# A decoder layer on one Trainium2 core: the opening of cross-attention, with the token normalisation on GpSimd instead of VectorE and four weight subtractions moved later

## The reference

```python
def _layernorm(x, axis=-1, eps=1e-05):
    m = jnp.mean(x, axis=axis, keepdims=True)
    v = jnp.var(x, axis=axis, keepdims=True)
    return (x - m) / jnp.sqrt(v + eps)
...
x = x + _L0_attn_ref(_layernorm(x), ...)
x = x + _L0_xattn_ref(_layernorm(x), ctx, ctx, pos, mask, Wq, Wk, Wv, Wo)
# inside _L0_xattn_ref
q = (query @ Wq).reshape(nb, q_len, H, D).transpose(0, 2, 1, 3)
q = q * cos + _rotate_half(q) * sin
scores = jnp.where(mask == 0, -1e9, (q @ k) / sqrt(D))
x = softmax(scores) @ v ... @ Wo
```

## Time and profile before

| | |
|---|---|
| median of 3 runs | 1502.08 us |
| lowest and highest run | 1494.2 and 1506.05 us |
| the profiled execution | 1500.9 us |
| its span, first to last instruction | 1499.1 us |
| mean granted TensorE clock | 0.981 of full speed |
| busy share of PE, DVE, POOL, ACT | 96%, 73%, 32%, 28% |

### The profile page before, as it was taken

One profiled execution on the slowest core, in us unless ns is written; L12 is line 12 of the kernel. 1 busy time (PEld: TensorE's weight loads), 2 busy tenths in 40 slices (PEclk: granted clock), 3 DMA queues, 4 the chain that ended last, 5 costly groups with the idle time before them and its releaser, 6 DMA issues.

```text
span 1499.1 us, 28421 instructions
## 1 busy us (share of the span) xinstructions
PE 1442.0 (96%) x11616; PEld 1164.0 (78%) x11616; DVE 1098.8 (73%) x1632; ACT 426.1 (28%) x742; POOL 484.7 (32%) x427
## 2 busy tenths in 40 slices
PE   7999999999995699999999999999999999999999
PEld 6788888788873577877877777777778878877787
DVE  3655552888895777787787787787787887888854
ACT  4211233665652212221221222222222221221421
POOL 4322210534331233433333333333333323332221
PEclk9999999999995789999999999999999999999999
DMA  7665320000003210020010020020020020001111
GB/s 240 191 190 174 102 74 2 16 10 17 10 2 114 59 40 29 29 57 29 29 63 24 29 69 24 22 71 22 22 71 27 18 71 29 15 29 38 74 49 64
DMA packets 79121, 84.14 MB, mean 56 GB/s; under 512 B 9824, under 2 KB 50928, under 8 KB 78736
## 3 DMA queue, kind: packets, MB, share of 16 engines
q1 hardware_dynamic: 68976, 63.42, 13.4%
q10 hardware_dynamic: 9216, 16.78, 3.6%
q0 software_dynamic: 800, 2.11, 0.5%
HBM read 59.22 MB, written 23.07 MB: 55 GB/s over the span
## 4 chain that ended last, share of the span: by engine, by line
PE 64%; DVE 2%; issue 1%; ACT 1%; DMA 0%; SPq 0%; ACTq 0%
PE p_ps_q L75 9%; PE p_ps_y L1087 8%; PE p_ps_q L76 8%; PE p_ps_q L77 8%; PE p_ps_y L1088 8%; PE p_ps_y L1089 8%; PE p_ps_s L1049 4%; PE p_ps_o L1074 4%; PE p_ps_p L1059 2%; PE p_ps_y L1668 1%; PE p_ps_y L1670 1%; PE p_ps_y L1669 1%; PE p_ps_o L156 1%; PE p_ps_q L1631 0%; DMA p_raw_q<-in_wq 0%
## 5 line engine op out<-in xcount | busy, mean ns | idle before, releaser
L1395 POOL TENSOR_TENSOR p_q_rot<-p_ra,p_rb 128x512 f32<-128x512 f32 x128 | 167.0, 1304 | 289.7 <-DVE p_rb L164 289.7
L1087 PE MATMUL p_ps_y<-p_wo_hi,p_o_hi 128*128 128x512 f32 x512 | 212.2, 414 | 1.5 <-DVE p_o_lo L1282 1.4
L75 PE MATMUL p_ps_q<-p_xt_hi,p_wq_hi 128*128 128x512 f32 x512 | 212.5, 415 | 0.0
L76 PE MATMUL p_ps_q<-p_xt_lo,p_wq_hi 128*128 128x512 f32 x512 | 203.9, 398 | 0.0
L1088 PE MATMUL p_ps_y<-p_wo_lo,p_o_hi 128*128 128x512 f32 x512 | 202.7, 396 | 0.0
L77 PE MATMUL p_ps_q<-p_xt_hi,p_wq_lo 128*128 128x512 f32 x512 | 202.5, 395 | 0.0
L1089 PE MATMUL p_ps_y<-p_wo_hi,p_o_lo 128*128 128x512 f32 x512 | 202.4, 395 | 0.0
L1387 POOL TENSOR_TENSOR p_pn<-p_p,p_inv 128x512 f32<-128x512 f32 x64 | 66.9, 1045 | 301.0 <-DVE p_inv L1262 301.0
L1183 ACT ACTIVATE p_o_hi<-p_ps_o 128x512 fp32r<-128x512 f32 x128 | 69.5, 595 | 277.1 <-PE p_ps_o L1074 275.7
L1292 DVE TENSOR_TENSOR x_sb<-p_ps_y,x_sb 128x512 f32<-128x512 f32 x128 | 88.0, 688 | 78.3 <-PE p_ps_y L1089 78.3
L162 DVE TENSOR_TENSOR p_ra<-p_ps_q,p_cos_t 128x512 f32<-128x512 f32 x128 | 85.9, 671 | 62.7 <-PE p_ps_q L77 59.5
(11 more groups left out here) (217 smaller groups left out, 2992.4 us busy)
## 6 DMA issues: line engine op xcount, KB each, us to landing
p_raw_q<-in_wq SPq DMA_DIRECT2D x36, 256.0 KB, 3.2
v_scratch<-p_v_out SPq DMA_DIRECT2D x32, 256.0 KB
k_scratch<-p_k_out SPq DMA_DIRECT2D x32, 256.0 KB, 2.1
p_k_t<-k_scratch ACTq DMA_DIRECT2D x32, 256.0 KB, 2.6
p_v_in<-v_scratch ACTq DMA_DIRECT2D x32, 256.0 KB, 2.8
p_raw_o<-in_wo SPq DMA_DIRECT2D x32, 256.0 KB, 3.8
x_sb<-in_x SPq DMA_DIRECT2D x16, 256.0 KB, 2.9
out<-p_y SPq DMA_DIRECT2D x16, 256.0 KB, 2.0
```

What stands on the lines that cost most here:

```text
L75: nc.tensor.matmul(out, lh, rh, start=(c == 0), stop=False)
L76: nc.tensor.matmul(out, lh, rl, start=False, stop=False)
L1087: nc.tensor.matmul(ps_y[t][:, :], oh, w_hi["o"][h][:, :], start=(h == 0), stop=False)
L1395: nc.gpsimd.tensor_tensor(q_rot[:, h, :], ra[:, :], rb[:, :], ALU.add).then_inc(q_added, 1)
```

## The change

The normalisation of the 16 tiles moves from DVE to POOL, as `normalise_tile(t)`, with the same waits, behind a wait of POOL for the norm's mean and reciprocal root. POOL's four `split_q_lo(0, h)` and its four `add_terms(0, h)` are put between the tiles: the splits behind tiles 1, 3, 7 and 11, the additions behind tiles 9, 12 and 15 and at the end. The four `split_o_lo(0, h)` leave their place ahead of `shift(0)`; two now stand between `invert(0)` and `rotate(1, 0)`, two between `shift(1)` and `invert(1)`.

```diff
--- before.py
+++ after.py
@@ -1294,16 +1294,9 @@
                     need(dve, y_added, n * UT + t + 1)
                     norm3.collect(nc, tile + t)
 
-            def norm(t):
-                need(dve, transposed, t - 1)
-                norm2.apply(nc, xn[t % 2], t).then_inc(xn_ready, 1)
-
             norm2.finish_vector(nc, dve)
-            norm(0)
             for b in range(NB):
                 for t in range(b * TPB, (b + 1) * TPB):
-                    if t + 1 < TILES:
-                        norm(t + 1)
                     need(dve, all_hi, t + 1)
                     nc.vector.tensor_tensor(xt_lo[:, :, t * P:(t + 1) * P], ps_t[t % 2][:, :].rearrange("p (c n) -> p c n", c=KC),
                                             xt_hi[:, :, t * P:(t + 1) * P], ALU.subtract).then_inc(all_lo, 1)
@@ -1318,16 +1311,20 @@
                     dve.wait_ge(masked, 1)
                     nc.vector.tensor_scalar(bound[:, :, :], bound[:, :, :], MASKED, None, ALU.add).then_inc(masked, 1)
             rotate(0, H - 1)
-            for h in range(H):
-                split_o_lo(dve, 0, h)
             dve.wait_ge(masked, 2)
             shift(0)
             for it in range(LAST):
                 n, g, b = 2 * it, it // NB, it % NB
                 outputs_lo(n - 1)
                 invert(n)
+                if it == 0:
+                    split_o_lo(dve, 0, 0)
+                    split_o_lo(dve, 0, 1)
                 rotate(it + 1, 0)
                 shift(n + 1)
+                if it == 0:
+                    split_o_lo(dve, 0, 2)
+                    split_o_lo(dve, 0, 3)
                 add(n - 1, 0)
                 invert(n + 1)
                 rotate(it + 1, 1)
@@ -1398,11 +1395,19 @@
                 need(pool, v_part, it + 1)
                 nc.gpsimd.tensor_tensor(v_lo[:, :], v_in[:, :], v_hi[:, :], ALU.subtract).then_inc(v_ready, 1)
 
-            for w, h in (("q", 0), ("q", 1), ("q", 2), ("q", 3), ("add", 0), ("add", 1), ("add", 2), ("add", 3)):
-                if w == "add":
-                    add_terms(0, h)
-                else:
-                    split_q_lo(pool, 0, h)
+            def normalise_tile(t):
+                need(pool, transposed, t - 1)
+                nc.gpsimd.tensor_scalar(xn[t % 2], x[:, t, :], norm2.mv[:, t:t + 1, 0], norm2.rstd[:, t:t + 1],
+                                        ALU.subtract, ALU.mult).then_inc(xn_ready, 1)
+
+            pool.wait_ge(norm2.norm, norm2.root_base + 1)
+            for t in range(TILES):
+                normalise_tile(t)
+                if t in (1, 3, 7, 11):
+                    split_q_lo(pool, 0, (1, 3, 7, 11).index(t))
+                if t in (9, 12, 15):
+                    add_terms(0, (9, 12, 15).index(t))
+            add_terms(0, 3)
             for it in range(ITS):
                 n, g, b = 2 * it, it // NB, it % NB
                 normalise_p(n)
```

## The result

| | before | after |
|---|---|---|
| median | 1498.2 us | 1511.37 us |
| profiled execution | 1500.9 us | 1509.43 us |
| ratio, with 95% interval | | 1.008 [1.0058, 1.0102] |

The change makes the kernel slower by 0.8%, some 12 us. One of the ten executions of each kernel lies far outside the others (6682.77 us before, 2027.31 us after, that one at 0.652 of the clock) and is left out of the ratio. The forecast was 1504.5, range 1496 to 1510, and "no change that can be measured". The direction of the sum was right (+2.4), its size was not. In the profiled executions the span grew from 1499.1 to 1507.6 us, by 8.5; the profiled execution of before was itself 2.7 above the median of its longer series.

What follows compares the result with a forecast made beforehand. PE was taken to bound the kernel, the change being worth what it moves mix(0). Terms 0 + 0.9 - 0.5 + 1.4 + 0.55 gave +2.35, say +2.4 us: median about 1504.5, range 1496 to 1510.

Steps and rivals of the forecast that it cites:

- What bounds the kernel: PE, busy 853.28 of 855.00 us after 545; a delay reaching it by then is carried to the end one for one.
- The price of the operation, 1.04 us: POOL's two-step normalisation of one 128x512 tile, taken from its broadcast multiply at 1.045; ends 0.52 and 1.26 us.
- Tiles 0 to 7, nothing: First eight normalisations on POOL: no loss, since PE's cadence of 1.13 us isn't shorter than 1.04; lead taken as 0.
- Tiles 8 to 11, +0.9: POOL's split waits for ACT ahead of tile 8; tile 11 +0.4 us at the high clock or +1.4 at the low.
- tile 13, still +0.9: POOL's head 1 addition, queued ahead, waits for the rotation and meets the mask; tile 13 +0.4 to +1.4 us, middle +0.9.
- Output weights: Four subtractions leaving shift(0): -0.5 us; first pair before rotate(1, 0): +1.4; second ahead of invert(1): +0.55.
- The queues: SP's loads of mask and weights start or land later but still before their use; nothing lost.
- The third rival: POOL's chain to tile 15, 484.0 + 16 d, decides from d = 1.75 us; 1512.5 at d = 2.30; chance 0.07.

Runs made afterwards that it cites:

- e3_pool_multiply: Changed kernel, same order, but POOL's operation per tile is one broadcast multiply by the reciprocal root, mean subtraction left out; 1.0031 of before.
- e4_four_forms: Changed kernel with four forms of POOL's operation, one or two steps, per-token scalars or constants, four tiles each; 2.07, 1.55, 1.91, 1.50 us, no kernel time claimed.
- e2_weights_only: Kernel before with only the four output-weight subtractions moved as in the change, normalisation still on DVE; 1.0027 of before.
- the control: Kernel before with one further wait on POOL for the norm's reciprocal, meant to move nothing in the opening; 0.9995 of before.
- e10_weights_free_place: Kernel before with only the four output-weight subtractions moved between outputs_lo(0) and rotate(1, 3); 1.0037 of before.
- e6_pool_order: Changed kernel with head 2's and 3's weight splits behind tiles 8 and 9, head 0's and 1's additions behind 10 and 14; scores(0) at 50.98, no time claimed.
- e9_reordered_dve: Kernel before, tiles 5, 9, 13 normalised ahead of rotations, mask behind rotate(0, 3), output-weight subtractions between outputs_lo(0) and rotate(1, 3); 0.9979 of before.

## Why the prediction was wrong, step by step

- **What bounds the kernel:** right. Nothing behind the opening changed (948.2 against 948.2), and what PE had lost at scores(2), 9.9 us, arrived at the end one for one.
- **The price of the operation, 1.04 us: wrong, and it is the step that failed.** 2.07 was measured, above the 1.75 that the prediction itself gave as a sign of being wrong. It was taken from the nearest row by size and by reading a broadcast, and both ends of its range, 0.52 and 1.26, came from other kinds of instruction. The range of the sum was made from these ends and so was too narrow. `e3_pool_multiply` shows that with the assumed price the first part costs nothing, and `e4_four_forms` which part of the price belongs to what.
- **Tiles 0 to 7, nothing:** wrong, and it follows from the price. PE came to tile 7 at 19.44 from the reciprocal, against 14.82 before: +4.6.
- **Tiles 8 to 11, +0.9, and tile 13, still +0.9:** the waits were where the prediction had them, for ACT ahead of tile 8 and for the rotation ahead of tile 13. Their size: tile 11 was 9.1 late (32.21 against 23.12), tile 13 10.7 (42.14 against 31.44). With the cheap form both were 0 and not +0.9: tile 11 stood at 23.05 and tile 13 at 31.42, so that not even the better end of the two clocks, +0.4, came true. Even with the right price these two terms were too dear.
- **Output weights:** the removal was to give -0.5 at scores(0). The addition of head 3 took 1.26 in `e2_weights_only`, as assumed, and 1.76 before. The landmark scores(0) alone doesn't show it, since the control has 45.14 too, with the subtractions in their old place; but from tile 15 to scores(0) it was 9.90 before, 9.87 in the control and 9.39 in `e2_weights_only`. The two pairs cost 1.52 at mix(0) (16.37 us from scores(0) before, 17.89 after; 1.96 against the control's 15.93), against 1.4 + 0.55. The first took 2.09 beside POOL, against 1.25 + 0.9. This part was right in the trace, to half a microsecond.
- **The queues:** in the changed kernel's opening (473 to 545 us) DVE and PE wait for no transfer. The one wait for one is ACT's for the first query weights, 2.8 us in all, the same as before. Right.
- **The third rival** (POOL becomes the bound) is what happened, with its chance set at 0.07. Its threshold, 1.75 us, was set too high: in `e4_four_forms` the four forms average 1.76 us, at which its formula would lose 0.2 us, and tile 15 was 9.3 us late (45.05 against 35.76). The true one lies between the 1.04 of `e3_pool_multiply`, where nothing was lost, and that. The formula holds POOL's busy time and none of its pauses. It gives 484.0 + 16 x 2.07 = 517.1, tile 15 late by 5.2; it was late by 10.6. Left out were POOL's pauses and meetings: 1.95 and 1.44 us of waits, 1.0 more for the addition beside the mask (2.29), 1.0 more for a normalisation (7.16 for three). These make 5.4, and the sum agrees. That its 1512.5 lies near the measured 1511.37 is luck: it was worked out for a price of 2.30 and without pauses.
- **The time against the trace.** The change costs 9.9 us at scores(2) against the trace of before, and 13.3 against the control's; the medians differ by 12 to 13. The one trace of before had the low clock behind mix(0), which not every execution has. So a comparison of two single executions here is uncertain by some 3 us, and the forecast's base was too.
- **The rest of the small losses.** `e2_weights_only`, `e3_pool_multiply` and `e10_weights_free_place` are 4 to 5 us slower in the median. Against the trace of before, their mix(0) moved by only 1.0, 1.0 and -1.3 us, and scores(2) by 0.5, 0.5 and 0.1. Against the control's trace, whose program has the median of before, scores(2) moved by 3.9, 3.9 and 3.5, nearly the whole of it. For `e2_weights_only` 2.0 of the 3.9 had been lost at mix(0); the other 2.0 is PE's clock behind it, 12.25 us at 0.79 for what the control did in 10.30:

```profile
541.38:553.63 12.25, 12.25 (x52) 9.64 (x53) 6.81 (x10) 1.69 (x3) 3.04 (x3) 0.79 0.14 43
```

- **Open:** why the low clock stands behind mix(0) in some executions. In the five traces in which PE had idled 3.8 to 4.9 us ahead of mix(0), the clock up to scores(2) was 0.76 to 0.85; in the seven with 2.5 to 2.6 us it was 0.75 to 1.00, in three of these with a further wait in between. A longer wait may bring the low clock more often; one profile each can't show this, and it wasn't tried.

## What to carry to other kernels

A price from another kind of instruction is no bound, not even one with the same engine, size and more operands: where no row shows the operation, the range has to reach to where that engine becomes the bound, and that point has to be worked out with its waits, not from its busy time alone. Before work goes to an idle engine, ask for that engine's price of this very instruction; here 0.50 us on DVE, 0.81 on ACT and 2.07 on POOL for the same tile. And an idle gap in one execution may be the shadow of another engine's clock: it isn't there in each execution.

## What the runs showed of the hardware

- POOL's `tensor_scalar` of 128x512 takes 1.50 to 2.07 us, its `tensor_tensor` with a broadcast 1.04 and with two full inputs 1.26. The instruction that reads one tensor less is the slower one.
- POOL's addition beside DVE's two mask operations took 2.29 or 2.30 us in nine of the ten traces with the mask in its old place, against 1.26 alone, and DVE's second mask operation 2.17 against 1.23 for the first. The tenth is `e6_pool_order`: there a normalisation on POOL met the first mask operation (2.30 and 1.33 us) and the addition began 0.4 us after the second (2.23 and 1.51). So the second operation's 2.17 is not its own price.
- With the mask behind the last rotation (`e9_reordered_dve`) the two met POOL's addition of head 3, which took 2.30 us again. The addition of head 2, while DVE stood idle, took 1.26. Here are DVE's rows of the meeting:

```profile
517.18 1.23 DVE L1318 TENSOR_SCALAR b_bound<-b_bound 128x2048 f32<-128x2048 int32 x1
518.45 2.17 DVE L1320 TENSOR_SCALAR b_bound<-b_bound 128x2048 f32<-128x2048 f32 x1
```
